# A state-space scan in a four-layer kernel: in layer 2, every second state step's inputs are formed on GpSimd instead of VectorE

## The reference, cut to what matters

```python
# _L2_attn_ref, per batch element; x_main, dt: (512, 256); Bm, Cm: (512, 16); A: (256, 16)
dt = softplus(dt_raw @ W_dt.T + b_dt);  A = -exp(A_log)
h  = exp(dt_t[..., None] * A) * h + dt_t[..., None] * B_t[:, None, :] * x_t[..., None]
y  = einsum('ben,bn->be', h, C_t)
y  = (y + x_main * D_param) * silu(z);  out = y @ W_out.T + residual;  layernorm(out)
# _L2_ffn_ref: logits -> top 2 of 8 -> softmax weights; y = xt + sum_e w[e] * (silu(xt @ we1[e] + be1[e]) @ we2[e] + be2[e])
```

## Time and profile before

| | |
|---|---|
| time, median of 3 runs (lowest to highest) | 1404.84 us (1404.35 to 1404.96) |
| the profiled execution: its own time, its span | 1417.23 us, 1415.5 us |
| mean granted TensorE clock in it | 0.92 |
| PE busy over the span | 1155.0 us (82%) |
| DVE busy | 997.0 us (70%) |
| ACT busy | 761.7 us (54%) |
| POOL busy | 615.9 us (44%) |
| layer 2's 64 scans | from 761.5 to 1182.0 us of the span |

### The profile page before, as it was taken

One profiled execution on the slowest core, in us unless ns is written; L12 is line 12 of the kernel. 1 busy time (PEld: TensorE's weight loads), 2 busy tenths in 40 slices (PEclk: granted clock), 3 DMA queues, 4 the chain that ended last, 5 costly groups with the idle time before them and its releaser, 6 DMA issues. The chain is left out here.

```text
span 1415.5 us, 21028 instructions
## 1 busy us (share of the span) xinstructions
PE 1155.0 (82%) x7010; PEld 812.6 (57%) x7010; DVE 997.0 (70%) x2280; ACT 761.7 (54%) x1584; POOL 615.9 (44%) x607
## 2 busy tenths in 40 slices
PE   3999999998888786377966887888887778988885
PEld 1455665664564575266844555555555555777774
DVE  2476677669787654567737989989989997634445
ACT  1456556555545445244437686586767674344442
POOL 3244444544348824443101533633633753136661
PEclk9999999999999898588978998998999999789997
DMA  7400000000000033810000000000000000001113
GB/s 174 117 1 1 1 1 1 1 1 1 1 8 24 30 89 102 253 35 16 1 12 0 1 1 1 1 1 0 1 1 1 1 1 14 18 17 39 40 38 105
DMA packets 54443, 40.71 MB, mean 29 GB/s; under 512 B 13185, under 2 KB 46687, under 8 KB 54337
## 3 DMA queue, kind: packets, MB, share of 16 engines
q1 hardware_dynamic: 40994, 27.58, 6.8%
q0 software_dynamic: 4544, 9.32, 2.4%
q10 hardware_dynamic: 8800, 2.48, 0.9%
HBM read 26.32 MB, written 13.04 MB: 28 GB/s over the span
## 5 line engine op out<-in xcount | busy, mean ns | idle before, releaser
L780 POOL TENSOR_TENSOR PR<-PR,R 128x512 f32<-128x512 f32 (+3 forms) x128 | 160.6, 1266 | 231.7 <-DVE R L1275 231.2
L1980 POOL TENSOR_TENSOR YY<-YY,H 128x512 f32<-128x512 f32 x120 | 164.3, 1392 | 187.6 <-DVE H L2430 187.6
L410 PE MATMUL banks<-XT,we 128*128 128x128 f32 (+1 forms) x568 | 175.2, 440 | 11.9 <-ACT HH L2252 10.5
L1074 ACT ACTIVATE PR<-banks,NM 128x257 f32<-128x257 f32 (+3 forms) x256 | 132.4, 527 | 94.8 <-DVE NM L1247 93.0
L410 PEld LDWEIGHTS banks<-we,HH 128*128 128x128 f32 x1024 | 145.1, 205 | 35.4 <-issue 30.2
L2422 DVE TENSOR_TENSOR_SCAN H<-wide,H 128x1024 f32<-128x1024 f32 x64 | 164.4, 2568 | 0.2
L410 PE MATMUL banks<-we,HH 128*128 128x128 f32 x1024 | 145.5, 289 | 0.0
L410 PE MATMUL banks<-BCR,SEL 96*128 96x512 f32 x128 | 68.2, 535 | 76.4 <-DVE H L2430 65.1
L2252 ACT ACTIVATE HH<-banks,be1f 128x512 f32<-128x512 f32 x128 | 84.1, 687 | 83.5 <-PE banks L410 82.6
L410 PEld LDWEIGHTS banks<-XT,we 128*128 128x128 f32 x568 | 90.4, 202 | 65.3 <-issue 43.4
L410 PEld LDWEIGHTS banks<-PTS,V 128*64 128x64 f32 x1152 | 66.4, 139 | 84.1 <-issue 53.7
(11 more groups left out here) (564 smaller groups left out, 2447.5 us busy)
## 6 DMA issues: line engine op xcount, KB each, us to landing
xsort<-zrow SPq DMA_DIRECT2D x1, 3072.0 KB, 13.9
XS<-xsort SPq DMA_DIRECT2D x12, 256.0 KB, 2.9
ysort<-PTS SPq DMA_DIRECT2D x12, 256.0 KB, 2.2
pj_stage<-in_L_ffn_w_proj SPq DMA_DIRECT2D x1, 2048.0 KB, 12.0
we<-in_L_ffn_we SPq DMA_DIRECT2D x1, 2048.0 KB
we<-yrows SPq DMA_DIRECT2D x8, 256.0 KB, 5.4
xrows<-XN SPq DMA_DIRECT2D x4, 256.0 KB, 3.5
out<-XN SPq DMA_DIRECT2D x4, 256.0 KB, 2.3
```

The source lines that it names most:

```text
L410: return nc.tensor.matmul(o, l, r, start=start, stop=stop)
L780: last = nc.gpsimd.tensor_tensor(p, p, R[:, T * q + t, :].unsqueeze(2).to_broadcast([P, 2, w]), ALU.mult)
L1074: nc.scalar.activation(PR0[:, q % 2, s, OFF[t]:OFF[t] + w], ps2(n)[:, s, SLOT[t]:SLOT[t] + w], ACT.Exp, bias=NM[:, m, s:s + 1], accum_out= ...
L1980: nc.gpsimd.tensor_tensor(YY[:, m, :], YY[:, m, :] if n else XD[m], H[:, k % 4, m, :], ALU.add).then_inc(ya, 1)
```

## The change

For even k from 4 on, 30 of the 64 steps, `inputs(k)` leaves DVE. ACT copies row n of B out of bank 1 into the SBUF tile `BROW` (128 x 512; the tile XN, unused in layer 2) at the head of its iteration k-2, and POOL multiplies DTX by `BROW` into H[k % 4], in its iteration k-2, behind `add_y(k-3)`. `scan(k)` waits for POOL (`bmp`) at these steps, and `b_row(k+1)` waits for ACT's copy (`bc`) instead of for the product. The next copy waits for POOL's product before.

```diff
+            def by_pool(k):
+                return k >= 4 and k % 2 == 0
...
+                BROW = XN[:, :, :].rearrange(flat)
...
+                        def inputs(k):                                   # GpSimd
+                            b = k // NS
+                            g.wait_ge(bc, pool_steps(k))
+                            g.wait_ge(dtx, b + 1)
+                            g.wait_ge(ya, 2 * (k - 3))
+                            nc.gpsimd.tensor_tensor(H[:, k % 4, :, :], DTX[:, b % 2, :, :],
+                                                    BROW.unsqueeze(1).to_broadcast([P, 2, S]), ALU.mult).then_inc(bmp, 1)
...
                             add_y(k - 1)
+                            if k + 2 < NK and by_pool(k + 2):
+                                inputs(k + 2)
...
-                            if k:
-                                pe.wait_ge(bm, k)                        # b_row on TensorE
+                            if k and by_pool(k - 1):
+                                pe.wait_ge(bc, pool_steps(k - 1))
+                            elif k:
+                                pe.wait_ge(bm, dve_steps(k - 1))
...
+                        def copy_row(k):                                 # ScalarE
+                            act.wait_ge(bp, k + 1)
+                            if pool_steps(k) > 1:
+                                act.wait_ge(bmp, pool_steps(k) - 1)
+                            nc.scalar.activation(BROW, PS[:, 1, :], ACT.Copy).then_inc(bc, 1)
...
                             more = b + 1 < B
+                            if k + 2 < NK and by_pool(k + 2):
+                                copy_row(k + 2)
...
-                            v.wait_ge(bm, k + 1)                         # scan on VectorE
+                            if by_pool(k):
+                                v.wait_ge(bmp, pool_steps(k))
+                            else:
+                                v.wait_ge(bm, dve_steps(k))
...
-                            if k + 2 < NK:
+                            if k + 2 < NK and not by_pool(k + 2):
                                 inputs(k + 2)
```

More of the change, by code:

```diff
@@ L1885, in layer2, with pool_steps, dve_steps @@
             LAST = NK - 1
+            bmp, bc = lsem("a2_inputs_by_pool"), lsem("a2_b_rows_copied")
+            def by_pool(k):
+                return k >= 4 and k % 2 == 0
+            def pool_steps(k):
+                return sum(by_pool(i) for i in range(k + 1))
+            def dve_steps(k):
+                return k + 1 - pool_steps(k)
             uses = {}
```

## The result

The changed kernel takes 1439.7 us (median of 4 runs, 1439.48 to 1441.9) against 1404.9 for the kernel before (4 runs, 1404.35 to 1406.78): a ratio of 1.0243, 95% interval 1.0223 to 1.0263. It is slower by 34.8 us; 1432 was forecast, with a range of 1409 to 1452.

What follows compares the result with a forecast made beforehand. DVE was taken to bound layer 2's scan, busy 395.96 of 421 us. Added waits, net of the 33.9 us saved, summed to 27.9 on the median 1404.8: 1432.7 us, range 1409 to 1452.

Steps and rivals of the forecast that it cites:

- n = 0: Pair of iterations 0 and 1: `gated` waits for POOL's late addition and the product, +2.4 three times, 7.2 us.
- n = 12: Pair holding iteration 13: two additions and a product's end fall between three instructions, +1.0 three times, 3.0 us.
- n = 10: Iterations 10 and 11: +0.6 three times, 1.8 us, the wait for ACT hiding the rest.
- n = 2: Behind the gate's chain, POOL's product goes ahead of `scan(19)`: +1.0 four times, 4.0 us.
- n = 4: Behind `out_stats`, the product goes ahead of the scan and POOL's small instructions come late: +1.05 three times, 3.2 us.
- n = 6: An addition and the product get between `finish`'s four instructions: +1.3, +2.2, +1.5, and +0.3 without `finish`, 5.3 us.
- the light pairs: Some 10 pairs without further work win nothing: 0 to 0.5 us slower each, 2 us in all.
- The product takes 2.5 us: POOL's new 128 x 1024 product, both inputs in SBUF: 2.5 us taken, 1.90 as lower bound.
- Rival 2: ACT's row copy over 5 us late delays product, scan and `b_row(k+3)`; each microsecond costs 30: 1450 to 1480, 5%.
- Rival 3: Additions of light pairs pile up on POOL and `gated` waits for all of them: 1445 to 1460, 14%.
- Rival 1: POOL's product runs beside DVE's work: whole saving kept, 1371, 5%; in part, 1395 to 1409, 8%.
- Signs named: L2415 at 34 executions, 30 POOL products of 2.5 to 4.7 us, scans' mean about 3200 ns, `gated` over 3 us.

Runs made afterwards that it cites:

- e3: Changed kernel with two memsets of H in place of each GpSimd product, all waits and row copies kept: 1400.3 us, ratio 0.9942 to the kernel before.
- e1: Kernel before plus extra GpSimd products of 128 x 768 from SBUF that nobody waits for, VectorE's program untouched: 1422.7 us, ratio 1.0097.
- e2: Kernel before plus two GpSimd memsets of 128 x 768 in place of each extra product, writing SBUF and reading nothing: 1408.2 us, ratio 0.9998.
- e5: Changed kernel with GpSimd's product split into two instructions of 128 x 512: 1428.7 us, ratio 1.0144 to the kernel before.
- e6: Changed kernel with inputs(18), (34) and (50) back on VectorE, 27 products staying on GpSimd: 1427.7 us, ratio 1.014 to the kernel before.
- e9: Kernel before with only inputs(20), (36) and (52) moved to GpSimd, placed while VectorE waits for the gate: 1407.3 us, ratio 1.0.
- e8: Changed kernel with only inputs(6), (22), (38) and (54) on GpSimd, 26 back on VectorE: 1409.2 us, ratio 1.0023 to the kernel before.
- e4: Changed kernel without ScalarE's row copies and the waits on them, GpSimd multiplying by a constant row: 1436.2 us, ratio 1.0195 to the kernel before.
- e11: Kernel before with inputs(20), (36), (52) on GpSimd during the gate wait, and some add_y second halves delayed until after the scan: 1401.9 us, ratio 0.9961.

## Why the prediction was right

The direction and the mechanism hold, and of the seven terms in the table two (n = 0 and n = 12) hold place by place. n = 10 was too low, n = 2 was mis-sized, n = 4 and n = 6 are wrong in ways that cancel in part, and the light pairs' sum agrees by luck. That the whole came out at 34 us for 28 owes something to this luck.

1. *A scan and a two-input instruction on POOL exclude each other, PSUM readers don't.* Shown by e3 (some 40 us back without the reads), by e1 against e2, and by e5 for the whole instruction. The Trainium skill's rule (SBUF — State Buffer, section "Who interferes with whom") agrees with it, also in that a GpSimd instruction which only writes doesn't contend with a VectorE instruction that has two SBUF inputs: e2's memsets left the scans at 2566 ns. The page's exemption of VectorE instructions with one SBUF input is for those outside its 2-port modes; the prediction left that condition out, and the last point of this document shows a copy with one SBUF input that was held up.
2. *The product takes 2.5 us.* It took 2.37, or 2.34 straight behind an addition. The estimate of 2.25 from the Trainium skill (GPSIMD Engine Reference, section 3.1) was about as far off, on the other side. The light pairs at n = 14 came to 10.90 to 10.92, one with a queue (k = 60) to 11.23, where 11.09 and 11.42 were stepped. Their sum, +2.9 for 3.4, is another matter: the pair at k = 56, forecast +1.4, came out at -1.7, the last step at -0.95, and the pair at k = 58 at +3.3, which no term foresaw.
3. *`gated` loses 2.4 three times:* 2.24. *n = 12:* +1.0 forecast, 0.96 measured. *n = 10:* 2.9 for 1.8, from places of +1.9, -0.7 and +1.7; the +0.6 was none of them.
4. *n = 2: +1.0 four times* is the mis-sized term: 11.7 us in place of 4.0. The scan's wait itself was right, +1.00 in the first batch element, which has no gate, and +0.95 to +0.99 in the rest of the pair in the others. The step that failed is that I held the chain over PE and ACT to the gate fixed at 8.95 us. It took 7.31 to 9.96 before and 11.32 now, 7.7 us more over three places. e6, which removes the stall before it, takes 1.2 to 1.6 off each, all of it in the chain. That the granted clock falls because PE stands still longer is what this and the order of events suggest; but e9 in three places and e8 in one had the same 0.55 behind PE's old wait of 2.44 us, so the stall is not its only cause. And since the chain already varies by 3 us between places and profiles of one VectorE program, the 7.7 is known only roughly.
5. *n = 4: +3.2* was wrong in sign, -2.8. The margin of 0.1 to 0.2 us went the other way because the row came late, by 0.57 us at b = 1 and 2 and 0.22 at b = 3, where I had put it 5 us early. The row is early in a light pair; behind `apply_in` on ACT it isn't. e4 restores the forecast. *n = 6: +5.3* measured 9.7 for the same reason: POOL comes later to four additions and a product, and `finish` on DVE, four instructions with two SBUF inputs, runs into them (7.40 us instead of 2.9 in two places).
6. *Rival 2, the row comes late:* it did, 26.5 us of POOL's waiting, but it cost 3 to 7 us by e4 and not 30 for each microsecond. *Rival 3, POOL as the pace:* the pair at k = 58 (14.35 instead of 11.07 us, DVE waiting 2.49 in the ring) looks like it; elsewhere POOL caught up. *Rival 1, the product beside DVE's work:* it didn't happen, and e3 suggests that even a product that blocks nothing would have won about 8 us in this order of work, not 34.
7. Signs named: L2415's successor has 34 executions, the product 30 with 2.34 to 4.37 us, `gated` over 3 us. The scans' mean rose to 2811 ns over all 64, not to 3200: 15.6 us in all and not 40. The rest of the loss is in DVE's other two-input instructions (`gated`, `finish`) and above all in 29.6 us more in which DVE stood still, 7.8 of them at the gate.

## What to carry to other kernels

- Before moving work from VectorE to GpSimd, count who reads two operands from SBUF. Here the product that reads PSUM stayed at 1.21 us on VectorE whatever GpSimd did; on GpSimd it competed with the scans and the other two-input instructions. That turned 34 us saved into 35 lost.
- Shortening one instruction on a busy engine changes what the next one meets. Step one period through on both engines with starts and ends, and look for margins under 0.3 us: each is a place where the forecast can change its sign.
- Don't hold a chain over other engines fixed when you delay what starts it: the one to the gate went from 7.3 to 10.0 us to 11.3.
- If the work must go there, cut it into short instructions (e5, 14 us) and fit the ones that block into gaps (e11, 0.4 to 0.6% better than before, with no less work on GpSimd).

## What I had not expected of the hardware

- In every place that I looked at, a waiting VectorE instruction came ahead of GpSimd's next one, even with four additions queued (5.0 us of additions took 8.95 with two scans between).
- GpSimd's recorded times hold the wait: 2.37 us undisturbed, 4.37 behind a scan. Read alone they look like a slow instruction.
- A copy on VectorE with one SBUF input was affected too. `split`'s cast of 32 x 512 took 0.42 us before, with nothing on POOL beside it, and in the changed kernel 0.42 once and 1.56 twice, with additions beside it. In e2 it took 0.80 us three times, beside a memset of 0.74 that had started 0.2 ahead of it. So this instruction, unlike the scan, waits also for a GpSimd instruction that only writes:

```profile
L2417 DVE CAST BCR<-XNT 32x512 fp32r<-32x512 f32 x3 | 3.5, 1181 | 0.1
```
